# Cross network for a recommendation tower: x0 three times goes to PSUM, VectorE ends the fold, ScalarE builds the diagonals

## The chip, the cores and the metric

One core of a Trainium2 chip runs the whole kernel. The metric is the device time of one execution in microseconds (us), lower is better. The kernel before takes 761.69 us (median of three runs, 758.12 to 764.24).

## What is computed

Batch B=512, F=39 fields, D=16 embedding columns, M=128 filters per layer. Rows are gathered from 39 tables, then three cross layers multiply the input with the layer's output and contract over pairs, and a small top network follows:

```
e = stack([tbl_f[ids[:, f]] for f in range(39)], axis=1)        # 512 x 39 x 16
x0 = xk = e
for W in (f0, f1, f2):
    z = einsum('bfd,bgd->bfgd', x0, xk).reshape(b, f * g, d)
    xk = einsum('bpd,pm->bmd', z, W); outs.append(xk)
z = sum(concatenate(outs, axis=1), axis=-1)                      # 512 x 384
h = relu(concatenate([z, dense_ctx], axis=1) @ W_top1 + b_top1)
y = relu(h @ W_top2 + b_top2) @ W_top3
```

## The kernel before, in words

The 512 x 16 pairs of batch row and column d are 8192 positions, worked on in 16 **tiles** of 512 (32 batch rows each). Four tiles make a group of 128 batch rows.

**Gathers.** GpSimd gathers by indirect DMA: nine "quads" (four, three or two fields in one transfer, from a table of all small fields, `quad`, L400) per tile, and seven "singles" (`single`, L391) per group, issued in the third and fourth tile ahead of the group. SyncE stores them turned to a DRAM scratch `x0_dram` (`store_singles`, `store_quad`), then loads x0 stacked three times (`three`, `x0_three`, 117 x 512) and shifted copies of x0 into `z` (`turned_rows`), two tiles ahead.

**Layer 1** of tile t+1 is made while tile t is in layer 2, in seven chunks of three shifts each, one every fourth slot from slot 0: VectorE's `product` (L616) multiplies `z` by `x0_three`, ScalarE's `high_part` rounds the result to the matmul's type, GpSimd's `low_part` (L411) subtracts it from the product, TensorE's `contract` (L716, L717, L722) adds three matmuls per chunk into the PSUM bank `acc0`, eight slots behind the product. Then come `x1_high` and `x1_low` (L622), and the sum over d (`sum_x1`, L629).

**Layer 2** has 640 **banks**: a tile is four blocks of 128 positions, and a block ten banks (`BANKS`), one per **slot** of the code's loop. TensorE's `layer2` (L740 to L742) writes a bank of four fields x 128 filters (three in the last) to one of `RING` = 5 PSUM tensors `y2`, with three matmuls. Banks 0, 3 and 6 of each block are scaled by x0 on ScalarE (`scale_bank`, L500, four instructions), the other seven on VectorE (`add_bank`, L646, 27 instructions per block), which adds them onto one of ScalarE's three results `scaled`. TensorE may write bank n when bank n-5 has been read.

**The fold.** GpSimd adds the three parts of `scaled` (`fold_two`, L417, and the first addition of `finish_x2`, L424), halves the result twice (L426, L430) and so has `x2_sb` of the block. TensorE's `s_block` (L747) multiplies `x2_sb` by `diag`, a block-diagonal of x0 made by VectorE's `spread_rows` (L654), two instructions per tile, at slots 2 and 12. ScalarE copies the outcome to `s_sb`; `rows_of` and `rows` (L706, then L469) turn x0 to rows for it and for the scaling.

**Layer 3 and the top** of a group run on TensorE in the slots of the next group: `layer3` (L758) in slots 10 to 131 of its 160, `top1` to `top3` from slot 137 on, that is in its fourth tile. The last group's stand alone after the last bank.

Every engine's order is written out by hand in slots, and semaphores carry all dependencies. At the start `keep_warm` (L791) issues 26 matmuls that serve no result, and the two filter parts are split into high and low parts (ScalarE L469, VectorE L662, L675).

## Time and profile before

| | us |
|---|---|
| median of three runs | 761.69 |
| the profiled execution | 761.12 |
| its span, first to last instruction | 759.2 |
| around the span | 1.9 |
| first matmul of layer 2 | 49.2 |
| last bank's first matmul | 729.2 |
| mean granted TensorE clock, as a share of full speed | 0.973 |

Tile t lies between its first layer-2 matmul (L740) and the next tile's. These starts are, in us: 49.2, 97.7, 141.1, 181.4, 221.8, 267.0, 311.7, 352.4, 396.5, 441.7, 486.5, 527.2, 571.2, 612.6, 653.4, 692.3. In the profile DVE is VectorE, ACT is ScalarE, POOL is GpSimd, PE is TensorE's matmuls and PEld its weight loads. Matmuls are pipelined and each one's end is modelled, so PE's busy time overstates how little room is left.

### The profile page before, as it was taken

How to read it: one execution, taken by the hardware profiler on the slowest of the kernel's cores; microseconds unless marked ns; L12 is line 12 of the kernel's file. 1: busy time of each engine (PE TensorE's matmuls, PEld its weight loads, DVE VectorE, ACT ScalarE, POOL GpSimd, SP SyncE). 2: the span in 40 equal slices, each digit the busy share in tenths (PEclk: the TensorE clock that was granted, in tenths of full speed). 3: DMA queues.
4: the chain of work that ended last, by engine and by line, in shares of the span. 5: the costliest groups of instructions: out<-in, count | busy, mean ns of one | idle time of the engine just before them, and what ended most of it. 6: DMA issues, size and time to landing. Idle time of an engine off the chain costs nothing.

```text
span 759.2 us, 11476 instructions
## 1 busy us (share of the span) xinstructions
PE 684.3 (90%) x3058; PEld 530.7 (70%) x3058; DVE 638.4 (84%) x1981; ACT 335.4 (44%) x1019; POOL 589.1 (78%) x540
## 2 busy tenths in 40 slices
PE   0587888999999898999999898999999999999977
PEld 0365665767676676868886676877887687878856
DVE  4669798898989798998979799798969999999650
ACT  1333443544544444444544444444455454544421
POOL 6468889798989889797979979797968989574430
PEclk9979999999999999999999999999999999999989
DMA  9628220303030210303030120303031030300000
...
DMA packets 69746, 41.25 MB, mean 54 GB/s; under 512 B 46913, under 2 KB 54529, under 8 KB 69554
## 3 DMA queue, kind: packets, MB, share of 16 engines
...
q8 instruction: 24, 0.39, 0.2%
q14 instruction: 40, 0.33, 0.1%
...
## 4 chain that ended last, share of the span: by engine, by line
PE 35%; POOL 24%; DVE 24%; issue 13%; DMA 2%; SPq 1%; ACT 0%; POOLq 0%; DVEq 0%
DVE scaled L646 17%; PE y L740 7%; POOL emb_quads L400 7%; PE y L741 6%; PE y L742 6%; POOL z_parts L411 5%; POOL sum L424 4%; POOL sum L417 3%; PE late L758 3%; POOL sum L426 3%; DVE z L616 3%; PE side L747 2%; PE side L706 2%; DVE diag L654 2%; PE acc L722 2%
## 5 line engine op out<-in xcount | busy, mean ns | idle before, releaser
L646 DVE SCALAR_TENSOR_TENSOR scaled<-y,x_rows,scaled 128x128 f32<-128x128 f32 x1728 | 462.8, 338 | 72.1 <-PE y L742 49.3
L740 PE MATMUL y<-w_hi,x_parts 128*128 128x512 f32 (+1 forms) x640 | 281.9, 440 | 12.4 <-DVE scaled L646 8.6
L500 ACT ACTIVATE scaled<-y,x_rows 128x128 f32<-128x128 f32 x768 | 218.2, 367 | 149.3 <-PE y L742 148.5
L741 PE MATMUL y<-w_lo,x_parts 128*128 128x512 f32 (+1 forms) x640 | 251.4, 393 | 0.0
L742 PE MATMUL y<-w_hi,x_parts 128*128 128x512 f32 (+1 forms) x640 | 251.1, 392 | 0.0
L400 POOL DMA_INDIRECT emb_quads<-in_small_tables_dram,quad_rows x144 | 153.3, 1065 | 26.4 <-issue 18.7
L740 PEld LDWEIGHTS y<-w_hi,x_parts 128*128 128x128 f32 x640 | 122.7, 192 | 66.0 <-DVE scaled L646 42.2
L411 POOL TENSOR_TENSOR z_parts<-z,z_parts 117x512 fp32r<-117x512 f32 (+1 forms) x108 | 140.0, 1296 | 26.3 <-ACT z_parts L469 25.1
L469 ACT ACTIVATE z_parts<-z 117x512 fp32r<-117x512 f32 (+1 forms) x112 | 70.7, 632 | 162.7 <-DVE z L616 162.7
L742 PEld LDWEIGHTS y<-w_hi,x_parts 128*128 128x128 f32 x640 | 122.6, 192 | 25.2
L741 PEld LDWEIGHTS y<-w_lo,x_parts 128*128 128x128 f32 x640 | 123.4, 193 | 17.4 <-issue 0.4
L616 DVE TENSOR_TENSOR z<-z,x_three 117x512 f32<-117x512 f32 (+1 forms) x112 | 120.3, 1076 | 5.2 <-DMA z<-x_turned 5.2
L424 POOL TENSOR_TENSOR sum<-sum,scaled 128x512 f32<-128x512 f32 x64 | 88.0, 1375 | 32.8 <-DVE scaled L646 32.2
L417 POOL TENSOR_TENSOR sum<-scaled 128x512 f32<-128x512 f32 x64 | 83.0, 1297 | 36.9 <-DVE scaled L646 36.6
L722 PE MATMUL acc<-z_parts,w_hi 117*128 117x512 f32 (+1 forms) x112 | 48.8, 436 | 22.7 <-POOL z_parts L411 21.8
L758 PEld LDWEIGHTS late<-s_sb,w_sb 128*128 128x128 f32 x312 | 55.1, 200 | 11.8 <-ACT s_sb L469 1.5
L758 PE MATMUL late<-s_sb,w_sb 128*128 128x128 f32 x312 | 56.5, 285 | 0.5 <-ACT s_sb L469 0.5
L426 POOL TENSOR_TENSOR sum<-sum 128x256 f32<-128x256 f32 x64 | 52.9, 827 | 5.0
L430 POOL TENSOR_TENSOR x_sb<-sum 128x128 f32<-128x128 f32 x64 | 48.7, 761 | 9.0
L747 PE MATMUL side<-diag,x_sb 128*128 128x320 f32 x128 | 47.9, 456 | 7.8 <-issue 6.2
L469 ACT ACTIVATE s_sb<-side 128x320 f32<-128x320 f32 x64 | 27.7, 433 | 58.1 <-PE side L747 58.0
L722 PEld LDWEIGHTS acc<-z_parts,w_hi 117*128 117x128 f32 (+1 forms) x112 | 22.0, 196 | 37.6 <-POOL z_parts L411 32.1
...
## 6 DMA issues: line engine op xcount, KB each, us to landing
...
x_turned<-emb_quads SPq DMA_DIRECT2D x160, 8.0 KB
...
x_turned<-emb_singles SPq DMA_DIRECT2D x64, 2.0 KB
...
```

The lines of the kernel that those rows point to most:

```text
L400: pool.indirect_dma_start(out=emb_quads[0:SPT * n, u % 2, i, :], out_offset=None, in_=packed, in_offset=bass.IndirectOffsetOnAxis(ap=quad_ ...
L411: pool.tensor_tensor(z_lo[0:k, n % Z_RING, :], z[0:k, c, :], z_hi[0:k, n % Z_RING, :].bitcast(F32), ALU.subtract).then_inc(z_lo_in, 1)
L417: pool.tensor_tensor(sum4[:, :], scaled[:, k % 2, 0, :], scaled[:, k % 2, 1, :], ALU.add).then_inc(four_in, 1)
L424: pool.tensor_tensor(sum4[:, :], sum4[:, :], scaled[:, k % 2, 2, :], ALU.add).then_inc(four_in, 1)
L469: return act.activation(dst, src, ACT.Copy)
L500: done = act.activation(scaled[:, k % 2, BY_ACT.index(j), i * M:(i + 1) * M], y2[n % RING][:, i * M:(i + 1) * M], ACT.Copy, scale=x0_rows[ ...
L616: dve.tensor_tensor(z[0:k, c, :], z[0:k, c, :], x0_three[0:k, u % 2, :], ALU.mult).then_inc(prod, 1)
L646: dve.scalar_tensor_tensor(part, y2[n % RING][:, i * M:(i + 1) * M], x0_f, part, ALU.mult, ALU.add).then_inc(terms_in, 1)
L740: pe.matmul(dst, x1_hi[:, t % 2, cols], hi, start=True, stop=False)
L741: pe.matmul(dst, x1_hi[:, t % 2, cols], lo, start=False, stop=False)
L742: pe.matmul(dst, x1_lo[:, t % 2, cols], hi, start=False, stop=True).then_inc(y_ready, 1)
L758: mm = pe.matmul(late[:, 0:P], w2_sb[:, f, :], s_sb[:, g % 2, f, :], start=f == 0, stop=f == F - 1)
```

## The change

- **Products from PSUM.** ScalarE copies `x0_three` of a tile to a new PSUM tensor `three_ps` (`three`, at slot 38 two tiles ahead, for tile 1 at slot 2 of tile 0), and `product` multiplies `z` by it. PSUM has eight banks, so the ring `y2` has four tensors in place of five.
- **The fold.** GpSimd's two halvings go. VectorE's `x2_of` reduces `sum4` over its four parts, with one `tensor_reduce` whose inner step is 128 elements, at slot 4 of the next block.
- **Diagonals.** VectorE's `spread_rows` goes. ScalarE writes one 32-partition piece of the diagonals at each of eight slots, into one of two buffers that VectorE zeroes once.
- **Gathers.** Two singles, fields 36 and 38, become parts of quads: five singles per group. SyncE's stores per tile rise from 19 to 22.
- **The start.** `w1` is loaded ahead of `w0` (three quarters of it on ScalarE's queue), ScalarE splits `w1` first, VectorE's last two cuts of `w1_lo` come after `sum_x1(0)`, `keep_warm` issues 30, and 2 more after each of five of tile 0's contractions.

The heart of the diff:

```diff
-QUADS = ((0, 4), (5, 4), (9, 4), (13, 4), (17, 3), (21, 4), (25, 4), (29, 2), (32, 3))
-SINGLES = (4, 20, 31, 35, 36, 37, 38)
+QUADS = ((0, 1, 2, 3), (5, 6, 7, 8), (9, 10, 11, 12), (13, 14, 15, 16), (17, 18, 19, 36),
+         (21, 22, 23, 24), (25, 26, 27, 28), (29, 30, 38), (32, 33, 34))
+SINGLES = (4, 20, 31, 35, 37)
...
-RING = 5
+RING = 4
...
-FINISH_AT = 2
+THIRD_AT = 2
+X2_AT = 4
...
-DIAG_AT = (2, 12)
+THREE_AT = 38
+FIRST_THREE_AT = 2
+DIAG_AT = (1, 2, 4, 5, 7, 8, 10, 11)
...
             def fold_two(k):
                 pool.wait_ge(terms_in, dve_terms(BANKS * k + BY_ACT[2] - 1))
+                if k > 0:
+                    pool.wait_ge(x2_in, k)
                 pool.tensor_tensor(sum4[:, :], scaled[:, k % 2, 0, :], scaled[:, k % 2, 1, :],
                                    ALU.add).then_inc(four_in, 1)
...
-                pool.wait_ge(four_in, 2 * k + 2)
-                pool.tensor_tensor(sum2[:, :], sum4[:, 0:2 * M], sum4[:, 2 * M:4 * M], ALU.add).then_inc(two_in, 1)
-                if k >= 2:
-                    pool.wait_ge(s_ready, k - 1)
-                pool.wait_ge(two_in, k + 1)
-                pool.tensor_tensor(x2_sb[:, k % 2, :], sum2[:, 0:M], sum2[:, M:2 * M], ALU.add).then_inc(x2_in, 1)
...
+            def spread_rows(t, b):
+                at = slice(32 * (b // 2), 32 * (b // 2) + 32)
+                if b == 0:
+                    act.wait_ge(rows_in, t + 1)
+                    if t >= 2:
+                        act.wait_ge(s_ready, NBLK * (t - 1))
+                act.activation(diag[at, t % 2, :, b, :], x0_rows[at, t % 2, :, :], ACT.Copy,
+                               scale=mask_sb[at, b:b + 1]).then_inc(diag_in, 1)
+
+            def three(u):
+                act.wait_ge(three_in[u % 2], 48 * (u // 2 + 1))
+                if u > 0:
+                    act.wait_ge(prod, C0 * u)
+                copy(three_ps[0:3 * F, :], x0_three[0:3 * F, u % 2, :]).then_inc(three_up, 1)
...
                 if c == 0:
-                    dve.wait_ge(three_in[u % 2], 48 * (u // 2 + 1))
+                    dve.wait_ge(three_up, u + 1)
...
-                dve.tensor_tensor(z[0:k, c, :], z[0:k, c, :], x0_three[0:k, u % 2, :], ALU.mult).then_inc(prod, 1)
+                dve.tensor_tensor(z[0:k, c, :], z[0:k, c, :], three_ps[0:k, :], ALU.mult).then_inc(prod, 1)
...
+            def x2_of(k):
+                dve.wait_ge(four_in, 2 * k + 2)
+                if k >= 2:
+                    dve.wait_ge(s_ready, k - 1)
+                dve.tensor_reduce(x2_sb[:, k % 2, :], sum4[:, :].rearrange("p (f m) -> p m f", f=FPB),
+                                  AX_X, ALU.add).then_inc(x2_in, 1)
...
             pe.wait_ge(quad_in[6][0], 16)
-            keep_warm(26)
+            keep_warm(30)
             for c in range(C0):
                 contract(0, c)
-                if c == 2:
+                if c == 4:
                     rows_of(0)
+                elif c < C0 - 1:
+                    keep_warm(2)
```

GpSimd's order, in the middle of a block of layer 2, before (`z_parts` is the low part of a product, `emb_quads` a gather, `sum` and `x_sb` the fold):

```order
L411 TENSOR_TENSOR z_parts<-z,z_parts 117x512 [waits z_done,z_hi_in]
L400 DMA emb_quads<-in_small_tables_dram,quad_rows 128x16
L424 TENSOR_TENSOR sum<-sum,scaled 128x512 [waits four_in,terms_in]
L426 TENSOR_TENSOR sum<-sum 128x256 [waits four_in]
L430 TENSOR_TENSOR x_sb<-sum 128x128 [waits two_in]
```

And the same place now, with the fold of the next block's first parts after it:

```order
L426 TENSOR_TENSOR z_parts<-z,z_parts 117x512 [waits z_done,z_hi_in]
L441 TENSOR_TENSOR sum<-sum,scaled 128x512 [waits four_in,terms_in]
L415 DMA emb_quads<-in_small_tables_dram,quad_rows 128x16
L426 TENSOR_TENSOR z_parts<-z,z_parts 117x512 [waits z_done,z_hi_in]
L415 DMA emb_quads<-in_small_tables_dram,quad_rows 128x16 x2
L434 TENSOR_TENSOR sum<-scaled 128x512 [waits x2_in,terms_in]
```

The two halvings (L426, L430 before) are gone, and the next `fold_two` now also waits for VectorE's `x2_in`.

VectorE's order from the first product of a tile in steady state, before (`scaled<-y_n` is one bank, n its PSUM tensor; `z<-z` a product; `diag` the diagonals):

```order
L616 TENSOR_TENSOR z<-z,x_three 117x512
L646 SCALAR_TENSOR_TENSOR scaled<-y_1,x_rows,scaled 128x128 x4
L646 SCALAR_TENSOR_TENSOR scaled<-y_2,x_rows,scaled 128x128 x4
L654 TENSOR_TENSOR diag<-x_rows,mask_sb 128x640
L646 SCALAR_TENSOR_TENSOR scaled<-y_4,x_rows,scaled 128x128 x4
L616 TENSOR_TENSOR z<-z,x_three 117x512
L646 SCALAR_TENSOR_TENSOR scaled<-y_0,x_rows,scaled 128x128 x4
```

And now:

```order
L652 TENSOR_TENSOR z<-z,three_ps 117x512
L682 SCALAR_TENSOR_TENSOR scaled<-y_1,x_rows,scaled 128x128 x4
L682 SCALAR_TENSOR_TENSOR scaled<-y_2,x_rows,scaled 128x128 x4
L682 SCALAR_TENSOR_TENSOR scaled<-y_0,x_rows,scaled 128x128 x4
L652 TENSOR_TENSOR z<-z,three_ps 117x512
L690 TENSOR_REDUCE x_sb<-sum 128x128
L682 SCALAR_TENSOR_TENSOR scaled<-y_1,x_rows,scaled 128x128 x4
```

The diagonals are gone from VectorE, and the reduction stands behind bank 4 and its product; the PSUM tensors come round after four.

VectorE's order at the start, before (`w_lo` of 128x896 first is `w0`, the rest `w1`):

```order
L599 TENSOR_SCALAR quad_rows<-ids_four 32x15 x32
L675 TENSOR_TENSOR w_lo<-s_sb,w_hi 128x896
L662 TENSOR_TENSOR w_lo<-s_sb,w_hi 128x1024 x4
L662 TENSOR_TENSOR w_lo<-s_sb,w_hi 128x896
L616 TENSOR_TENSOR z<-z,x_three 117x512 x2
```

And now:

```order
L635 TENSOR_SCALAR quad_rows<-ids_four 32x15 x34
L706 TENSOR_REDUCE mask_sb<-ident 128x8
L708 TENSOR_TENSOR s_sb<-s_sb 128x896
L710 TENSOR_TENSOR w_lo<-s_sb,w_hi 128x896
L696 TENSOR_TENSOR w_lo<-s_sb,w_hi 128x1024 x3
L652 TENSOR_TENSOR z<-z,three_ps 117x512 x2
```

The sum of the two `w0` parts has moved behind the row numbers of the gathers, and two of the five cuts of `w1_lo` no longer stand ahead of the products.

## Rows read from the trace of the kernel before

**Rows 1.** The page's part 1: busy us, share of the span, instructions.

```profile
PE 684.3 (90%) x3058; PEld 530.7 (70%) x3058; DVE 638.4 (84%) x1981; ACT 335.4 (44%) x1019; POOL 589.1 (78%) x540
```

**Rows 2.** Windows, tiles 0, 3, 4, 5, 7, 14, 15: window, length, busy (x), clock, DMA, GB/s.

```profile
49.20:97.70 48.50, 40.21 (x155) 30.07 (x156) 40.73 (x117) 19.42 (x60) 39.09 (x38) 0.93 0.52 158
...
181.40:221.80 40.40, 38.33 (x160) 27.72 (x159) 37.99 (x121) 19.95 (x62) 36.03 (x33) 1.00 0.20 51
...
221.80:267.00 45.20, 41.63 (x176) 31.45 (x176) 39.60 (x123) 20.20 (x63) 40.18 (x38) 0.96 0.21 52
267.00:311.70 44.70, 41.48 (x184) 32.50 (x184) 39.21 (x121) 19.89 (x61) 37.62 (x35) 0.96 0.20 51
...
352.40:396.50 44.10, 44.10 (x221) 35.76 (x220) 37.90 (x119) 21.86 (x70) 35.87 (x33) 1.00 0.24 60
...
653.40:692.30 38.90, 38.66 (x185) 31.35 (x183) 37.08 (x120) 19.90 (x61) 26.26 (x23) 1.00 0.05 14
...
692.30:729.20 36.90, 36.90 (x187) 30.37 (x186) 29.57 (x109) 17.01 (x60) 14.81 (x15) 1.00 0.00 1
```

**Rows 3.** Waits within tile 5 (267.0 to 311.7 us): total us, times, longest.

```profile
PE acc L722 <- POOL z_parts L411: 2.9, 2, 2.2
...
DVE scaled L646 <- PE y L742: 3.4, 2, 1.7
```

**Rows 4.** Waits within tile 14 (653.4 to 692.3 us).

```profile
DVE scaled L646 <- PE y L742: 1.7, 1, 1.7
...
PEld y L740 <- DVE scaled L646: 0.9, 2, 0.6
```

**Rows 5.** Groups of instructions, whole span: busy us, mean ns, idle before and releaser.

```profile
L646 DVE SCALAR_TENSOR_TENSOR scaled<-y,x_rows,scaled 128x128 f32<-128x128 f32 x1728 | 462.8, 338 | 72.1 <-PE y L742 49.3 <-ACT scaled L500 22.1
...
L616 DVE TENSOR_TENSOR z<-z,x_three 117x512 f32<-117x512 f32 (+1 forms) x112 | 120.3, 1076 | 5.2 <-DMA z<-x_turned 5.2
...
L426 POOL TENSOR_TENSOR sum<-sum 128x256 f32<-128x256 f32 x64 | 52.9, 827 | 5.0
...
L430 POOL TENSOR_TENSOR x_sb<-sum 128x128 f32<-128x128 f32 x64 | 48.7, 761 | 9.0
...
L654 DVE TENSOR_TENSOR diag<-x_rows,mask_sb 128x640 f32<-128x640 f32 x32 | 35.7, 1117 | 0.0
...
L391 POOL DMA_INDIRECT emb_singles<-in_tbl_dram,ids_sb x28 | 26.9, 959 | 8.9 <-issue 5.3 <-DMA ids_sb<-in_ids_dram 2.3 <-POOL sum L417 0.8
...
L622 DVE TENSOR_TENSOR x_parts<-acc,x_parts 128x512 fp32r<-128x512 f32 x16 | 10.9, 680 | 4.0 <-ACT x_parts L469 4.0
...
L629 DVE TENSOR_REDUCE r_sb<-acc 128x32 f32<-128x512 f32 x16 | 10.9, 680 | 0.0
```

**Rows 6.** Groups of instructions, ScalarE's copy of the 156 columns of rows.

```profile
L469 ACT ACTIVATE x_rows<-side 128x156 f32<-128x156 f32 x16 | 5.2, 325 | 1.5 <-PE side L706 1.5
```

**Rows 7.** Timeline of the start: start us, length us, what, idle before.

```profile
20.90 7.22 SPq L333 DMA_DIRECT2D x_turned<-emb_quads  x14
...
25.46 8.24 PE L791 MATMUL late<-w_hi 128*128 128x512 f32 x26 [25.46 <-DMA emb_quads<-in_small_tables_dram,quad_rows]
...
34.08 0.69 DVE L616 TENSOR_TENSOR z<-z,x_three 117x512 f32<-117x512 f32 x1 [3.08 <-DMA z<-x_turned]
...
52.28 0.39 PE L741 MATMUL y<-w_lo,x_parts 128*128 128x512 f32 x1
...
55.00 0.39 PE L741 MATMUL y<-w_lo,x_parts 128*128 128x512 f32 x1
...
56.51 0.69 DVE L616 TENSOR_TENSOR z<-z,x_three 117x512 f32<-117x512 f32 x1 [1.14 <-DMA z<-x_turned]
```

**Rows 8.** Windows, 40 to 45 us, in the order of rows 2.

```profile
40.00:45.00 5.00, 4.95 (x15) 3.89 (x15) 4.18 (x5) 1.97 (x4) 4.64 (x5) 0.50 0.08 7
```

**Rows 9.** Timeline of the end.

```profile
736.77 10.45 PE L758 MATMUL late<-s_sb,w_sb 128*128 128x128 f32 x78 [0.53 <-ACT s_sb L469]
```

**Rows 10.** Waits of the whole span, ScalarE for the products.

```profile
ACT z_parts L469 <- DVE z L616: 162.7, 105, 5.8
```

More of the change, by code:

```diff
@@ L38 @@
 CHUNKS = 12500
-QUADS = ((0, 4), (5, 4), (9, 4), (13, 4), (17, 3), (21, 4), (25, 4), (29, 2), (32, 3))
-SINGLES = (4, 20, 31, 35, 36, 37, 38)
-RUNS = ((0, 1), (1, 1), (2, 1), (3, 4))
+QUADS = ((0, 1, 2, 3), (5, 6, 7, 8), (9, 10, 11, 12), (13, 14, 15, 16), (17, 18, 19, 36),
+         (21, 22, 23, 24), (25, 26, 27, 28), (29, 30, 38), (32, 33, 34))
+SINGLES = (4, 20, 31, 35, 37)
 TURNED = 20
-QUAD_STORES = tuple(i for i, (f, n) in enumerate(QUADS) for _ in range(2 if f < TURNED else 1))
-STORES = len(QUAD_STORES) + len(RUNS) + sum(1 for i, n in RUNS if SINGLES[i] < TURNED)
 GATHER_AHEAD = 14
@@ L97, with runs @@
 W1_CUTS = (0, 8, 16, 24, 32, F)
+FIRST_CUTS = 3
+def runs(fields):
+    found = []
+    for i, f in enumerate(fields):
+        if found and found[-1][1] + found[-1][2] == f:
+            found[-1][2] += 1
+        else:
+            found.append([i, f, 1])
+    return [(i, f, n, (f, F + f) if f < TURNED else (f,)) for i, f, n in found]
+STORES = sum(len(at) for q in QUADS for _, _, _, at in runs(q)) + sum(2 if f < TURNED else 1 for f in SINGLES)
 def fields_of(j):
@@ L244, in cross_network @@
         late = ps("late", [P, COLS])
+        three_ps = ps("three_ps", [P, COLS])
         ids_in = sem("ids_in")
@@ L256, in cross_network @@
         mask_in = sem("mask_in")
+        no_diag = sem("no_diag")
         w0_sum = sem("w0_sum")
@@ L456, in _ @@
                         fold_two(k)
-                    if j == FINISH_AT and k > 0:
-                        finish_x2(k - 1)
+                    if j == THIRD_AT and k > 0:
+                        fold_three(k - 1)
                     for alone, a, i in gathers_at(t, s):
@@ L463, in _ @@
                             quad(a, i)
[L464 removed]
+            fold_three(BLOCKS - 1)
         @block.scalar
@@ L539, in _ @@
             act.wait_ge(four_ids_in, 64)
-            load_filter(act, 2)
-            load_filter(act, 3)
-            act.wait_ge(w0_sum, 1)
-            copy(w0_hi[:, :, :], w0_raw).then_inc(w0_hi_in, 1)
+            for a in range(1, 4):
+                load_filter(act, a)
             act.wait_ge(w1_in, 256)
@@ L547, in _ @@
                 copy(w1_hi[:, cut, :], w1_raw[:, cut, :]).then_inc(w1_hi_in, 1)
+            act.wait_ge(w0_sum, 1)
+            copy(w0_hi[:, :, :], w0_raw).then_inc(w0_hi_in, 1)
             act.wait_ge(stored[0], 16 * STORES)
@@ L550, in _ @@
                 turned_rows(act, 0, c)
+            three(0)
             for c in range(C0):
@@ L555, in _ @@
             x1_high(0)
+            act.wait_ge(mask_in, 1)
+            act.wait_ge(blank, 1)
+            act.wait_ge(no_diag, 1)
             for t in range(TILES):
@@ L573, in _ @@
                         rows(t + 1)
+                    if s in DIAG_AT:
+                        spread_rows(t, DIAG_AT.index(s))
+                    if t == 0 and s == FIRST_THREE_AT:
+                        three(1)
+                    if t + 2 < TILES and s == THREE_AT:
+                        three(t + 2)
                     if g > 0:
@@ L594, in quad_numbers @@
             def quad_numbers(tiles):
-                for i, (f0, n) in enumerate(QUADS):
-                    for j in range(n):
+                for i, fields in enumerate(QUADS):
+                    for j, f in enumerate(fields):
                         at = slice(SPT * j, SPT * j + SPT)
-                        done = dve.tensor_scalar(quad_rows[at, tiles, i], ids_four[at, tiles, f0 + j],
-                                                 small.index(f0 + j) * CHUNKS * ROWS, None, ALU.add)
+                        done = dve.tensor_scalar(quad_rows[at, tiles, i], ids_four[at, tiles, f],
+                                                 small.index(f) * CHUNKS * ROWS, None, ALU.add)
                 return done
@@ L685, in _ @@
             sum_x1(0)
+            for i in range(FIRST_CUTS, len(W1_CUTS) - 1):
+                second_filter_low(i)
             for t in range(TILES):
@@ L697, in _ @@
                         sum_x1(t + 1)
-                    if s in DIAG_AT:
-                        spread_rows(t, DIAG_AT.index(s))
+                    if s % BANKS == X2_AT and n > BANKS:
+                        x2_of(n // BANKS - 1)
+            x2_of(BLOCKS - 1)
         @block.tensor
@@ L735, in layer2 @@
                 f = fields_of(j)
+                if n < BANKS:
+                    pe.wait_ge(w1_lo_in, sum(1 for at in W1_CUTS[:-1] if at <= f[-1]))
                 cols = slice(k % NBLK * P, k % NBLK * P + P)
```

63 lines of the change are left out of this document (24 added, 39 removed).

## The prediction, made before the changed kernel ran

> **What bounds the kernel now.** I read the page's shares first [rows 1]: TensorE is busy 90% of the span, VectorE 84%, GpSimd 78%. No engine stands out, and the share says little, since stages differ. So I cut the span into its 16 tiles [rows 2]. Tiles 3, 14 and 15 take 40.4, 38.9 and 36.9 us, tiles 4 and 5 take 45.2 and 44.7. The reader is to look at GpSimd's busy time beside the length: 36.0 of 40.4 us in tile 3, 40.2 of 45.2 in tile 4, but only 26.3 of 38.9 in tile 14, which has no gathers left to issue. Tile 14 makes a following tile and runs layer 3 like tile 5, and takes 5.8 us less. What differs is GpSimd's work: tiles 4 and 5 lie where a group's singles are gathered and quads are dense behind them. Tile 7 is another case: TensorE is busy for all of it (44.1 of 44.1), because the top network is added there.
>
> How GpSimd's lateness reaches the others is seen in the waits of tile 5 [rows 3]: TensorE waits 2.9 us for a low part of a product, and VectorE then waits 3.4 us for TensorE. After such a gap TensorE's granted clock is 0.96 as the mean of tiles 4 and 5, that is, a piece of them runs at 1.2 GHz and not 2.4 GHz; in tiles 3 and 14 it is 1.00 [rows 2]. In tile 14 VectorE waits 1.7 us only [rows 4]. So tiles 1 to 6, 8 to 10, 12 and 13 are bound by GpSimd together with VectorE, tiles 7 and 11 by TensorE, tile 14 by VectorE (37.1 busy of 38.9) with TensorE close behind, tile 15 by TensorE.
>
> **GpSimd's part of the change.** The two halvings go: 0.83 + 0.76 us per block [rows 5], 6.4 us per tile for four blocks; about 101.6 us in all. Two singles in seven go too: 0.96 us each [rows 5], 8 in all. Tile 3's 36.0 us fall to 29.6, tile 4's 40.2 to some 33. Both are then far under the tile's length, so GpSimd's low parts come in time, as in tile 14. Its new wait, `fold_two` for the reduction of the block before, is free if that reduction at slot 4 comes ahead of slot 8; behind it in GpSimd's queue stand low parts and gathers.
>
> **VectorE's part.** Per tile it loses its two diagonals: 2 x 1.12 = 2.2 us [rows 5]. Its products take 1.08 us in the mean, though the subtraction L622, with one of its two inputs in PSUM and the same 512 columns, takes 0.68 [rows 5]; the first product of tile 0, before GpSimd's first low part, takes 0.69 too [rows 7]. I take the rest for a wait for GpSimd on the way to SBUF, and since the new product has one input in PSUM, 0.68: 7 x 0.40 = 2.8 us less (bounds: 0 if that reading is wrong, 2.8). It gains four reductions. The trace has no reduction with an inner step of 128 elements; L629, the same 512 elements in order from PSUM, takes 0.68 us [rows 5]. Lower bound 0.6 (the row less its overlap with the instruction before), upper bound twice the row, 1.36; I take the row's 0.68: 2.7 us more. Sum: 2.2 + 2.8 - 2.7 = 2.3 us less per tile. Tile 14 has no gathers to be in its products' way, so I take half the saving, 1.4, there: 37.1 - 2.2 - 1.4 + 2.7 leaves 36.2 us.
>
> The Trainium skill's page "Vector Engine (DVE) Microarchitecture Reference", section "Measured stream behaviour on trn2" with its paragraph "The SBUF access granule: adjacent pairs", speaks against this reduction: a port keeps its full rate only where consecutive elements come as adjacent pairs, and a stream that hops at every element costs 1.73 to 2.5 ns per column. An estimate from that page is 0.96 to 1.36 us for the 512 columns here, and by it the sum would be 4 x 0.28 = 1.1 to 4 x 0.68 = 2.7 us worse per tile. No row here shows it; it is the first rival's mechanism.
>
> **ScalarE's part.** It gains eight diagonal pieces of 160 columns, each at most the 0.33 us of its copy of 156 columns [rows 6], 2.6 us, and one copy of 512 columns, about 0.63 us. Its busy time goes from 19.9 to 23.1 us of a tile of about 39: hidden, because it mostly waits. Cost taken 0; up to 0.3 us for each piece that stands ahead of a scaled bank VectorE needs, 1 us per tile, at the upper end.
>
> **TensorE and the ring.** TensorE's own need: from one L741 at 52.28 to the one four banks on at 55.00 us lie 12 matmuls, 0.23 us each at full clock [rows 7]. Of the 120 layer-2 matmuls of a tile 12 have only 384 columns: 108 x 0.23 + 12 x 0.17 = 26.9 us; 21 for the contraction 4.8; transposes and diagonals about 3; layer 3 26 x 0.13 = 3.5 at most (78 take 10.5 in the tail [rows 9]). That is 34.7 without layer 3 and 37 to 38 with it. A ring of four leaves TensorE one bank less of lead. Not shown before; bounded by 0 and one bank of 0.7 us for each of a tile's seven products, 4.9 us; I take 0.2, near the lower end, since four banks are still 3.0 us of VectorE's work (a bank is 4 instructions of 462.8 / 1728 = 0.27 us [rows 5], and seven banks in ten are its own) and the disturbances (one product, one reduction, one contraction) are 0.7 us each.
>
> **The start.** Layer 2 begins at 49.2 us. TensorE contracts tile 0 at half clock (0.50 from 40 to 45 us [rows 8]), and the products begin at 34.08 [rows 7]. The new order saves GpSimd two gathers ahead of the quads, but splits `w0` last, so `keep_warm` can only begin at about 27 (an estimate: the quads are in at 25.46 [rows 7] and the loads with them, and two splits of some 1 us follow) and, with 30 matmuls after the 26 that took 8.24 us [rows 7], end near 36. Seven contractions of 0.7 us and the extra matmuls of 0.46 give 44, then 1.3 us for the x1 parts: layer 2 begins near 45.5. Much of that is lost again, since tile 1's data set the pace: the first product of tile 1, at 56.5 and waiting for its DMA [rows 7], cannot come much sooner than two or three microseconds less, and now ScalarE stands at slot 2 for the stacked x0 and does bank 3 behind it. I take 54.8. SyncE's three more stores cost 0 to 1.5 us here (7.22 us for 14 [rows 7]) and are in it. The rest of tile 0 took 97.7 - 56.5 = 41.2 and falls like a loaded tile, to 36.5: tile 1 begins at 91.3 instead of 97.7.
>
> **The sum.** Tiles 1 to 3 (no layer 3): 38.1 each, VectorE's 36 us and the 2 us by which tile 14 exceeds its bound; 114.3. The nine tiles 4 to 6, 8 to 10 and 12 to 14: tile 14's 38.9 as it stands, with all of VectorE's saving there given to TensorE's need, plus 0.2 for the ring, 39.1 each; 351.9. Tiles 7 and 11: 43.5 each, as TensorE bounds them; 87.0. Tile 15: 36.8. Together 590.0, against 631.5 before. The tail from the last bank, 30.0 us, has one reduction of 0.68 in place of two halvings, whose means together are 1.59 but which nothing disturbs there: 29.8. So 91.3 + 590.0 + 29.8 = 711.1 us of span, and with 1.9 around it 713.0, against 761.12 of the profiled execution. That execution stands 0.6 us under the median of 761.69, which is nothing: 713.
>
> **Rivals.** *The reduction on VectorE takes the place of GpSimd's work* (0.17). Either it is slow by its stride, or VectorE stands at slot 4 until GpSimd's second addition is done. For it: both engines are full in the first 26 slots of a tile. Against it: from a block's last term to the reduction VectorE has three banks, over 3 us, and GpSimd needs 1.3 for its addition. What stands behind the waiting reduction are banks 5 to 9 of the next block, for whose release TensorE's ring waits, and the next product, for which ScalarE waits. 
>
> *GpSimd was not the bound* (0.10): its waits are symptoms and only VectorE's 2.3 us and the start count: 761 - 16 x 1.5 = 737 with TensorE taking part of it.
>
> *The ring of four decides, and it gets slower* (0.05). ScalarE waits 105 times for a product [rows 10], 1.55 us each, and a bank of its own is stuck behind each wait. If, with one PSUM tensor fewer, TensorE stood one bank, 0.7 us, at each, that is 74 us: 713 + 74 = 787. It decides from 48 / 105 = 0.46 us per wait on. Against it: in tile 14, where VectorE is nearly full, TensorE's loads wait 0.9 us in all for its releases [rows 4]. The Trainium skill's "TensorE: Matmul & The Clock Gate", in "A second HAM failure mode: psum-queue depth-cycling", reports that small stalls from cycling PSUM banks let the clock swing between its levels; of the tiles 3, 4, 5, 7 and 14, with the same ring, it was lower only in 4 and 5 [rows 2].
>
> *The loads come late* (0.06): the copy to `three_ps` waits at slot 38 for its DMA in each tile. SyncE's chain is 3 stores longer, but GpSimd's gathers come sooner. Behind the copy stands bank 0 of the next tile, which VectorE's bank 1 needs. 1 us for each of 14 tiles: 727.
>
> **How the numbers follow.** The forecast has 0.62. The lower end is TensorE's need alone in the nine tiles (38 instead of 39.1, 10 us) and 0.6 us less in the others (4 us), a start 2 us better: 713 - 10 - 4 - 2 = 697. The upper end takes in the first, second and fourth rivals with some of the ring: 741. A difference under 1% is about what a measurement of this kernel cannot tell from none: faster by more 0.92 (the forecast and all rivals but that of the ring, less 0.03 of their tails), within 0.05 and slower 0.03 (the ring's case, half of it milder than its price, and those tails).
>
> **What would show it.** Right: GpSimd busy about 30 us per tile; products at 0.68 us; tiles 4 and 5 as long as tile 12; clock 1.00 in them; no wait of TensorE for L411's successor. Wrong: a reduction over 0.9 us or a VectorE wait on GpSimd's sum in front of it (first rival); TensorE waiting for VectorE's or ScalarE's releases several us per tile instead of tile 14's 0.9 (third); tiles 4 and 5 still longer than 12 (second); ScalarE waiting for `x_three` (fourth).

## The result and the profile after

The changed kernel takes 734.37 us (median of four runs, 733.42 to 735.52), the kernel before beside it 760.22. The ratio is 0.9654, with a 95% interval of 0.9623 to 0.9686: 3.5% faster. Forecast were 713.0 us within 697 to 741.

The page's part 1 of the changed kernel, against [rows 1]:

```profile
PE 671.3 (91%) x3072; PEld 523.1 (71%) x3072; DVE 626.0 (85%) x2018; ACT 390.5 (53%) x1163; POOL 459.2 (63%) x404
```

GpSimd's share fell from 78% to 63%, ScalarE's rose from 44% to 53%, and TensorE and VectorE are each a point fuller. By tile, the windows of the changed kernel (tiles 0, 3, 4, 5, 7, 14 and 15, columns as in [rows 2]):

```profile
54.10:99.90 45.80, 38.87 (x156) 29.05 (x156) 38.03 (x121) 23.44 (x70) 34.93 (x32) 0.93 0.55 162
...
176.20:215.20 39.00, 37.91 (x159) 27.51 (x158) 37.55 (x122) 23.14 (x70) 28.64 (x26) 1.00 0.22 51
215.20:255.10 39.90, 38.96 (x176) 30.15 (x176) 37.79 (x122) 23.69 (x71) 30.83 (x28) 1.00 0.21 48
255.10:294.90 39.80, 39.23 (x184) 31.43 (x184) 37.61 (x122) 23.37 (x70) 28.79 (x26) 1.00 0.25 58
...
334.60:380.30 45.70, 45.13 (x220) 35.51 (x219) 37.76 (x122) 25.43 (x78) 28.51 (x26) 1.00 0.21 51
...
625.10:664.80 39.70, 39.22 (x185) 31.48 (x183) 37.45 (x122) 22.89 (x69) 19.03 (x16) 1.00 0.01 2
664.80:704.20 39.40, 38.59 (x188) 29.84 (x187) 32.99 (x114) 20.17 (x68) 9.54 (x9) 1.00 0.00 1
```

Tiles 4 and 5 took 45.2 and 44.7 us and now take 39.9 and 39.8, as long as tile 14, and the clock in them is 1.00, not 0.96. GpSimd is busy for 31 and 29 of these 40 us. So far that is the forecast, but for 0.6 to 0.8 us per tile (39.1 was forecast). And tile 14 got longer (38.9 to 39.7), tile 7 from 44.1 to 45.7 and tile 15 from 36.9 to 39.4, and tile 0 begins at 54.1 us, not 49.2. The groups of instructions, against [rows 5] and [rows 6]:

```profile
L682 DVE SCALAR_TENSOR_TENSOR scaled<-y,x_rows,scaled 128x128 f32<-128x128 f32 x1728 | 465.4, 342 | 53.5 <-PE y L781 35.6 <-ACT scaled L526 17.2
...
L441 POOL TENSOR_TENSOR sum<-sum,scaled 128x512 f32<-128x512 f32 x64 | 83.1, 1299 | 36.8 <-DVE scaled L682 36.3
...
L652 DVE TENSOR_TENSOR z<-z,three_ps 117x512 f32<-117x512 f32 (+1 forms) x112 | 75.6, 677 | 0.0
...
L690 DVE TENSOR_REDUCE x_sb<-sum 128x128 f32<-128x512 f32 x64 | 68.7, 1073 | 2.3 <-POOL sum L441 2.1
...
L496 ACT ACTIVATE diag<-x_rows,mask_sb 32x160 f32<-32x160 f32 x128 | 48.6, 416 | 1.2
...
L480 ACT ACTIVATE three_ps<-x_three 117x512 f32<-117x512 f32 x16 | 9.9, 617 | 7.8 <-DMA x_three<-x_turned 7.8
```

The product fell from 1.08 to 0.68 us, as forecast. The reduction L690 takes 1.07 us, not 0.68, and a diagonal piece L496 0.42, not 0.33. From the waits of tile 15 of the changed kernel (TensorE's weight loads waiting for VectorE: us in all, times, the longest):

```profile
PEld y L779 <- DVE scaled L682: 3.4, 8, 0.9
```

The same wait in tile 15 of the kernel before:

```profile
PEld y L740 <- DVE scaled L646: 0.2, 1, 0.2
```

TensorE's weight loads, which hardly waited for VectorE there (0.2 us), now wait 3.4 us. And the start of the changed kernel, from the timeline, against [rows 7]:

```profile
20.65 6.26 DVE L635 TENSOR_SCALAR quad_rows<-ids_four 32x15 int32<-32x15 int32 x34 [10.98 <-DMA ids_four<-in_ids_dram]
...
26.94 0.29 DVE L706 TENSOR_REDUCE mask_sb<-ident 128x8 f32<-128x128 f32 x1
...
33.42 9.39 PE L830 MATMUL late<-w_hi 128*128 128x512 f32 x30 [33.42 <-DVE w_lo L710]
...
49.17 0.30 ACT L480 ACTIVATE x_rows<-side 128x156 f32<-128x156 f32 x1 [4.93 <-PE side L743]
...
54.31 2.21 DVE L696 TENSOR_TENSOR w_lo<-s_sb,w_hi 128x1024 fp32r<-128x1024 f32 x2
```

VectorE stands until 20.65 us for the ids of the other tiles, whose load now lies behind a quarter of `w1`; the first sum and splits of `w0` are behind its 34 small additions, so the 30 matmuls begin at 33.42 (25.46 before). At 49.17 ScalarE has waited 4.9 us for the transposes, with the last two chunks of tile 0 queued behind them. Then, in tile 0 (ScalarE, then VectorE):

```profile
62.38 0.60 ACT L480 ACTIVATE three_ps<-x_three 117x512 f32<-117x512 f32 x1 [5.52 <-DMA x_three<-x_turned]
```

```profile
64.15 1.13 DVE L682 SCALAR_TENSOR_TENSOR scaled<-y,x_rows,scaled 128x128 f32<-128x128 f32 x4 [5.55 <-ACT scaled L526]
65.19 0.68 DVE L652 TENSOR_TENSOR z<-z,three_ps 117x512 f32<-117x512 f32 x1
```

ScalarE waits 5.5 us at slot 2 for tile 1's stacked x0, bank 3 comes after it, and VectorE waits 5.6 us for bank 3: the first product of tile 1 starts at 65.2 us, against 56.5 before.

The span is 733.7 us where 711.1 was forecast, 22.6 us more. Tile 1 begins at 99.9 instead of 91.3 (8.6 us more); tiles 1 to 3 take 115.3 instead of 114.3 (1.0); the nine tiles with layer 3, 39.66 to 39.92 each, 358.2 instead of 351.9 (6.3); tiles 7 and 11 together 91.4 instead of 87.0 (4.4); tile 15 39.4 instead of 36.8 (2.6); the tail 29.5 instead of 29.8.

### The profile page after: what moved, and what is told of

Its sections match the earlier page's. It is cut to its first block, busy times and chain, and to the rows that moved or that the text cites. A ratio compares the mean times of both kernels' runs of the same rounds, so it can differ in the third digit from the quotient of the medians.

```text
span 733.7 us, 11667 instructions
## 1 busy us (share of the span) xinstructions
PE 671.3 (91%) x3072; PEld 523.1 (71%) x3072; DVE 626.0 (85%) x2018; ACT 390.5 (53%) x1163; POOL 459.2 (63%) x404
## 4 chain that ended last, share of the span: by engine, by line
PE 67%; DVE 19%; issue 5%; DMA 3%; POOL 2%; ACT 2%; ACTq 1%; SPq 0%; DVEq 0%; POOLq 0%
PE y L779 17%; PE y L781 14%; PE y L780 14%; DVE scaled L682 14%; PE late L797 4%; PE side L786 3%; PE acc L754 3%; PE acc L753 3%; PE acc L759 3%; PE side L743 2%; DMA s_sb<-in_w_dram 2%; PE late L808 2%; DVE z L652 1%; PE late L830 1%; DVE x_parts L658 1%
## 5 line engine op out<-in xcount | busy, mean ns | idle before, releaser
L779 PE MATMUL y<-w_hi,x_parts 128*128 128x512 f32 (+1 forms) x640 | 277.7, 434 | 18.2 <-DVE scaled L682 8.8
L781 PE MATMUL y<-w_hi,x_parts 128*128 128x512 f32 (+1 forms) x640 | 249.0, 389 | 0.0
L780 PE MATMUL y<-w_lo,x_parts 128*128 128x512 f32 (+1 forms) x640 | 248.6, 389 | 0.0
L426 POOL TENSOR_TENSOR z_parts<-z,z_parts 117x512 fp32r<-117x512 f32 (+1 forms) x108 | 139.5, 1291 | 88.8 <-ACT z_parts L480 67.1
L779 PEld LDWEIGHTS y<-w_hi,x_parts 128*128 128x128 f32 x640 | 120.8, 189 | 80.8 <-DVE scaled L682 50.6
L415 POOL DMA_INDIRECT emb_quads<-in_small_tables_dram,quad_rows x144 | 138.0, 959 | 32.7 <-issue 15.5
L781 PEld LDWEIGHTS y<-w_hi,x_parts 128*128 128x128 f32 x640 | 120.7, 189 | 24.9
L441 POOL TENSOR_TENSOR sum<-sum,scaled 128x512 f32<-128x512 f32 x64 | 83.1, 1299 | 36.8 <-DVE scaled L682 36.3
L652 DVE TENSOR_TENSOR z<-z,three_ps 117x512 f32<-117x512 f32 (+1 forms) x112 | 75.6, 677 | 0.0
L690 DVE TENSOR_REDUCE x_sb<-sum 128x128 f32<-128x512 f32 x64 | 68.7, 1073 | 2.3 <-POOL sum L441 2.1
L496 ACT ACTIVATE diag<-x_rows,mask_sb 32x160 f32<-32x160 f32 x128 | 48.6, 416 | 1.2
L753 PE MATMUL acc<-z_parts,w_hi 117*128 117x512 f32 (+1 forms) x112 | 44.4, 396 | 0.9 <-ACT z_parts L480 0.9
L759 PE MATMUL acc<-z_parts,w_hi 117*128 117x512 f32 (+1 forms) x112 | 44.2, 395 | 0.7 <-POOL z_parts L426 0.7
```

Of the source, the lines that this page charges most:

```text
L415: pool.indirect_dma_start(out=emb_quads[0:SPT * n, u % 2, i, :], out_offset=None, in_=packed, in_offset=bass.IndirectOffsetOnAxis(ap=quad_ ...
L426: pool.tensor_tensor(z_lo[0:k, n % Z_RING, :], z[0:k, c, :], z_hi[0:k, n % Z_RING, :].bitcast(F32), ALU.subtract).then_inc(z_lo_in, 1)
L441: pool.tensor_tensor(sum4[:, :], sum4[:, :], scaled[:, k % 2, 2, :], ALU.add).then_inc(four_in, 1)
L652: dve.tensor_tensor(z[0:k, c, :], z[0:k, c, :], three_ps[0:k, :], ALU.mult).then_inc(prod, 1)
L779: pe.matmul(dst, x1_hi[:, t % 2, cols], hi, start=True, stop=False)
L780: pe.matmul(dst, x1_hi[:, t % 2, cols], lo, start=False, stop=False)
```

## The experiments

Theory A is the forecast's with its sizes mended: GpSimd's work bound the kernel, its removal is what pays, and the slow reduction, the ring of four and the new start give part of it back. The rivals are named in the expectations. The twelve kernels ran in three groups of four (1 to 4, 5 to 8, 9 to 12), each group beside the kernel before, whose medians were 757.87, 758.38 and 760.57 us. A ratio is to that median.

### 1. The ring alone, on the kernel before

```diff
-RING = 5
+RING = 4
```

> The kernel before with a ring of four PSUM tensors in place of five, nothing else. Theory A (the ring costs little, TensorE's lead of four banks is enough): 761 to 766 us. Theory B (the ring of four is what keeps the changed kernel above the forecast, since tiles 7 and 15 became 1.7 and 2.5 us longer there): 15 to 35 us more than before, about 775 to 795.

Measured: 755.62 us, ratio 0.9962 (0.9937 to 0.9987): 0.4% less, outside both expectations. The windows of its tiles 4, 14 and 15, and a wait within tile 15, show two effects of opposite sign:

```profile
219.70:263.30 43.60, 40.07 (x176) 29.78 (x175) 39.58 (x122) 20.23 (x63) 39.97 (x38) 1.00 0.20 46
646.50:686.10 39.60, 39.00 (x185) 31.47 (x183) 37.05 (x120) 20.09 (x61) 26.23 (x23) 1.00 0.05 14
686.10:723.70 37.60, 37.53 (x189) 29.93 (x187) 29.87 (x109) 17.00 (x59) 14.55 (x16) 1.00 0.00 1
```

```profile
PEld y L740 <- DVE scaled L646: 1.4, 5, 0.5
```

Tile 14 takes 39.6 (38.9 before) and tile 15 37.6 (36.9), and tiles 7 and 11 take 44.7 (44.0): 0.7 us more in each of the four tiles in which TensorE or VectorE and not GpSimd is the bound; in tile 15 TensorE's loads wait 1.4 us for VectorE, against 0.2. But tile 4 takes 43.6 in place of 45.2, at a clock of 1.00 and not 0.96 [rows 2]. That gain goes with the clock: in executions with the same mean clock both kernels take about the same time (spans of 753.1 to 754.9 us with four tensors and 753.7 with five at 0.984; 756.4 and 754.1 to 756.6 at 0.980), as far as these few executions tell; but with four tensors the mean clock was 0.980 to 0.989, and 0.966 to 0.982 with five beside it. How the ring acts on the clock was not tried. So theory B falls as the explanation of the 20 us. The 0.7 us per tile are real, and the changed kernel, whose clock is 1.00 from tile 1 to tile 15, has no such gain to set against them.

### 2. GpSimd's halvings alone

The fold's last addition of 512 columns goes straight to a buffer, and the diagonals multiply its first 128 columns; three quarters of x2 are left out.

```diff
-                pool.tensor_tensor(sum4[:, :], sum4[:, :], scaled[:, k % 2, 2, :], ALU.add).then_inc(four_in, 1)
-                pool.wait_ge(four_in, 2 * k + 2)
-                pool.tensor_tensor(sum2[:, :], sum4[:, 0:2 * M], sum4[:, 2 * M:4 * M], ALU.add).then_inc(two_in, 1)
+                pool.tensor_tensor(x2_sb[:, k % 2, :], sum4[:, :], scaled[:, k % 2, 2, :], ALU.add).then_inc(four_in, 1)
...
-                pool.tensor_tensor(x2_sb[:, k % 2, :], sum2[:, 0:M], sum2[:, M:2 * M], ALU.add).then_inc(x2_in, 1)
```

> The kernel before without GpSimd's two halvings, the diagonals multiply the first quarter of the sum (this leaves out three quarters of the block's x2). Theory A (GpSimd bound tiles 1 to 6, 8 to 10, 12 and 13): tiles 4 and 5 fall from 45 to about 41 us, the time falls by 20 to 30 us to about 735. Theory C (GpSimd's waits were only symptoms): within 5 us of before.

Measured: 712.83 us, ratio 0.9382 (0.9345 to 0.9419). That is 45 us, one and a half times the upper end of what I expected and more than the whole change brought. Its tiles 4 and 5, and its products:

```profile
206.60:246.50 39.90, 38.73 (x177) 30.60 (x177) 38.28 (x123) 20.23 (x63) 33.70 (x29) 1.00 0.20 48
246.50:286.00 39.50, 38.66 (x184) 31.43 (x183) 37.79 (x121) 19.91 (x61) 31.34 (x27) 1.00 0.23 58
```

```profile
L614 DVE TENSOR_TENSOR z<-z,x_three 117x512 f32<-117x512 f32 (+1 forms) x112 | 100.1, 895 | 4.0 <-DMA z<-x_turned 3.9
```

Tiles 4 and 5 are 5.3 and 5.2 us shorter than [rows 2], with VectorE's diagonals still there, the ring still five and the products still from SBUF. Of tile 4's 5.3 us, 1.6 are what it lost in experiment 1 too, where its clock rose to 1.00, and VectorE is busy for 1.3 us less (39.6 to 38.3), since its products fell to 0.90 us in the mean by themselves; the trace behind experiment 6 shows why. TensorE's wait for a low part in tile 5, 2.9 us in [rows 3], is gone. So GpSimd's halvings held the kernel up in two ways, by coming ahead of its low parts and by lengthening VectorE's products. Theory C falls; the two ways were not taken apart.

### 3. The reduction with neighbouring elements

Wrong elements are added; their number, the output and the waits stay.

```diff
-                dve.tensor_reduce(x2_sb[:, k % 2, :], sum4[:, :].rearrange("p (f m) -> p m f", f=FPB),
+                dve.tensor_reduce(x2_sb[:, k % 2, :], sum4[:, :].rearrange("p (m f) -> p m f", f=FPB),
```

> The changed kernel, with VectorE's reduction reading four neighbouring elements for each result in place of four that lie 128 apart (so the wrong elements are added). Theory A (the inner step makes the reduction 1.07 us and not 0.68): the reduction takes 0.6 to 0.7 us, and the time falls by 5 to 20 us. Theory D (the reduction is slow because its input is in SBUF or for its 128 results): it stays at 1.07 us and the time at 734.

Measured: 721.21 us, ratio 0.9512 (0.9479 to 0.9546), 13.2 us under the changed kernel by the medians.

```profile
L690 DVE TENSOR_REDUCE x_sb<-sum 128x128 f32<-128x512 f32 x64 | 43.3, 677 | 2.1 <-POOL sum L441 1.8
```

```profile
PEld y L779 <- DVE scaled L682: 2.0, 5, 0.6
```

The first line is the reduction: 0.68 us, as the row of L629 in [rows 5]. The inner step alone made the difference, theory D falls. The second is the wait of TensorE's loads within tile 15, 2.0 us and not 3.4. VectorE had 64 x 0.40 = 25 us less to do, half of which reached the time: tiles 2 and 3 lost 1.6 us each, the nine with layer 3, where TensorE is nearly full, 0.5 to 0.6.

### 4. The loads and splits of before

The order of SyncE's and ScalarE's loads, of the sums and splits is that of the kernel before; `keep_warm` stays as changed.

```diff
-            load_filter(sp, 0)
...
+            load_filter(sp, 0)
+            load_filter(sp, 1)
...
-            for a in range(1, 4):
-                load_filter(act, a)
+            load_filter(act, 2)
+            load_filter(act, 3)
+            act.wait_ge(w0_sum, 1)
+            copy(w0_hi[:, :, :], w0_raw).then_inc(w0_hi_in, 1)
```

> The changed kernel with the loads and splits of the filters in the order of before (w0 first, all five cuts of w1_lo ahead of the products); keep_warm stays at 30 and 2. Theory A (the new order makes the start late, through the row numbers and the last split of w0): layer 2 begins at 45 to 49 us in place of 54.1 and the time falls by 3 to 8 us. Theory E (the start is bound by the gathers and stores): layer 2 begins at 52 to 54 and the time stays.

Measured: 735.24 us, ratio 0.9685 (0.9651 to 0.9719), the same as the changed kernel, as theory E had it. The start in its profile, then the window from 40 to 44 us:

```profile
25.99 9.15 PE L828 MATMUL late<-w_hi 128*128 128x512 f32 x30 [25.99 <-DVE w_lo L711]
36.40 0.60 ACT L481 ACTIVATE three_ps<-x_three 117x512 f32<-117x512 f32 x1 [7.19 <-DMA x_three<-x_turned]
38.44 0.80 PE L751 MATMUL acc<-z_parts,w_hi 117*128 117x512 f32 x1 [3.30 <-ACT z_parts L481]
```

```profile
40.00:44.00 4.00, 4.00 (x10) 3.13 (x10) 3.89 (x7) 1.86 (x3) 2.86 (x3) 0.50 0.33 56
```

The 30 matmuls begin 7.4 us sooner, but the stacked x0 of tile 0 lands only at 36.4, so the contractions begin at 38.4 (42.65 in the changed kernel). TensorE has stood for 3.3 us before them, and its granted clock from 40 to 44 us is 0.50, where the changed kernel has 1.00. With the wait for the transposes behind it, layer 2 begins at 52.7 us and tile 1 at 97.3, 1.4 and 2.6 us sooner; the tail gives 2.0 back (31.6 us against 29.6). The order of the loads alone is not the cause.

### 5. and 6. Products from SBUF, with a ring of four and of five

```diff
-                dve.tensor_tensor(z[0:k, c, :], z[0:k, c, :], three_ps[0:k, :], ALU.mult).then_inc(prod, 1)
+                dve.tensor_tensor(z[0:k, c, :], z[0:k, c, :], x0_three[0:k, u % 2, :], ALU.mult).then_inc(prod, 1)
```

and ScalarE's `three` with its waits gone (SyncE's load of `x0_three` waits for the products again, as in the kernel before); in the second also `RING = 5`.

> The changed kernel with the products reading x0 from SBUF as before (no copy to PSUM), ring of four kept. Theory A (with two inputs in SBUF a product waits for GpSimd, the less the emptier GpSimd is): products 0.85 to 0.95 us as in the run without the halvings (0.90), VectorE 1.5 us per tile busier, 738 to 750 us. Theory F (the copy to PSUM brings nothing once GpSimd has room): 734 or less.

> The same with a ring of five, the PSUM tensor freed by the missing copy. Theory A (the ring of four costs 0.7 us in each tile that TensorE bounds, as tiles 7, 14 and 15 of the kernel before with a ring of four show): 5 to 11 us under the run with four. Theory F, the copy is a bad trade for the fifth tensor: below 734 us. Theory A says the two nearly cancel: 730 to 742.

Measured: 752.59 us with four (0.9918, 0.9883 to 0.9953) and 744.66 with five (0.9798, 0.9754 to 0.9842). Both are slower than I expected at most (750 and 742) and worse than the changed kernel. The copy to PSUM is worth 18 us at equal ring, and the fifth tensor takes 8 of them back. In the groups of the run with four, the product and GpSimd's second addition:

```profile
L641 DVE TENSOR_TENSOR z<-z,x_three 117x512 f32<-117x512 f32 (+1 forms) x112 | 100.3, 897 | 1.7 <-DMA z<-x_turned 1.7
L440 POOL TENSOR_TENSOR sum<-sum,scaled 128x512 f32<-128x512 f32 x64 | 88.3, 1380 | 37.3 <-DVE scaled L671 36.7
```

With two SBUF inputs the product takes 0.90 us in the mean in place of 0.68, and GpSimd's additions suffer as well: 1.38 in place of 1.30. The mean hides two kinds of product. One of each from tile 5 of that run, with what GpSimd does at the time:

```profile
267.99 0.68 DVE L641 TENSOR_TENSOR z<-z,x_three 117x512 f32<-117x512 f32 x1
285.41 2.62 DVE L641 TENSOR_TENSOR z<-z,x_three 117x512 f32<-117x512 f32 x1
```

```profile
284.92 1.31 POOL L425 TENSOR_TENSOR z_parts<-z,z_parts 117x512 fp32r<-117x512 f32 x1
286.17 1.30 POOL L440 TENSOR_TENSOR sum<-sum,scaled 128x512 f32<-128x512 f32 x1
```

Of the run's 112 products, the 49 that overlap no addition or subtraction of GpSimd take 0.67 to 0.69 us. The 30 that take over 0.8 us overlap one, all of them. In the kernel before 76 of 112 take over 0.8, in the run without the halvings 40, and again all of these overlap one. In the changed kernel, whose products have one input in PSUM, 72 overlap such an instruction, and none takes more than 0.70. The Trainium skill's "SBUF — State Buffer", in "Who interferes with whom", says that a VectorE instruction with two SBUF inputs contends with a GpSimd instruction that reads SBUF. By that rule, the trace agrees.

The loss is not even. The profiled span is 15.2 us longer than that of the changed kernel, and tiles 1, 5 and 9 (41.8, 43.4 and 43.4 us, against 37.4, 39.8 and 39.8) have 11.6 of it: there some products meet two of GpSimd's instructions in a row, as above. The other tiles are at most 0.8 us longer.

### 7. The sum written transposed

```diff
-                pool.tensor_tensor(sum4[:, :], sum4[:, :], scaled[:, k % 2, 2, :], ALU.add).then_inc(four_in, 1)
+                pool.tensor_tensor(sum4_m[:, :].rearrange("p (m f) -> p f m", f=FPB),
+                                   sum4[:, :].rearrange("p (f m) -> p f m", f=FPB),
+                                   scaled[:, k % 2, 2, :].rearrange("p (f m) -> p f m", f=FPB),
+                                   ALU.add).then_inc(four_in, 1)
```

VectorE reduces `sum4_m` with neighbouring elements.

> The changed kernel, but GpSimd's second addition writes its sum with the four parts of a result side by side, so that VectorE's reduction reads neighbouring elements and the right ones are added. Theory A (only the inner step made the reduction slow; GpSimd has room for a slower write): reduction 0.68 us, time 719 to 724 us. Theory G (GpSimd's writes with a step of four elements take twice as long and VectorE waits for them): above 726.

Measured: 722.23 us, ratio 0.9518 (0.9482 to 0.9555).

```profile
L442 POOL TENSOR_TENSOR sum_m<-sum,scaled 128x512 f32<-128x512 f32 x64 | 83.9, 1311 | 36.4 <-DVE scaled L686 36.0
...
L694 DVE TENSOR_REDUCE x_sb<-sum_m 128x128 f32<-128x512 f32 x64 | 43.4, 678 | 2.1 <-POOL sum_m L442 1.8
```

The write with a step of four elements costs GpSimd nothing to speak of (1.31 us, 1.30 in the changed kernel), and the reduction takes 0.68. Theory G falls.

### 8. Two additions in place of the reduction

```diff
-                dve.tensor_reduce(x2_sb[:, k % 2, :], sum4[:, :].rearrange("p (f m) -> p m f", f=FPB),
-                                  AX_X, ALU.add).then_inc(x2_in, 1)
+                dve.tensor_tensor(sum2[:, :], sum4[:, 0:2 * M], sum4[:, 2 * M:4 * M], ALU.add).then_inc(two_in, 1)
+                dve.wait_ge(two_in, k + 1)
+                dve.tensor_tensor(x2_sb[:, k % 2, :], sum2[:, 0:M], sum2[:, M:2 * M], ALU.add).then_inc(x2_in, 1)
```

> The changed kernel with VectorE's reduction replaced by two additions, 256 and 128 columns. Theory A: 0.40 and 0.27 us with some waits for GpSimd since both inputs are in SBUF, together 0.7 to 1.0 us against 1.07, time 722 to 732. Theory G (waits for GpSimd eat it): 734 or more.

Measured: 734.68 us, ratio 0.967 (0.9632 to 0.9708), no gain. The two additions:

```profile
L692 DVE TENSOR_TENSOR sum<-sum 128x256 f32<-128x256 f32 x64 | 43.9, 686 | 1.5 <-POOL sum L443 1.4
...
L694 DVE TENSOR_TENSOR x_sb<-sum 128x128 f32<-128x128 f32 x64 | 20.1, 314 | 2.2
```

Together 1.00 us, against 1.07. Two of the first additions, and GpSimd's instruction beside the second:

```profile
301.76 0.42 DVE L692 TENSOR_TENSOR sum<-sum 128x256 f32<-128x256 f32 x1
310.59 1.63 DVE L692 TENSOR_TENSOR sum<-sum 128x256 f32<-128x256 f32 x1
```

```profile
310.63 1.30 POOL L428 TENSOR_TENSOR z_parts<-z,z_parts 117x512 fp32r<-117x512 f32 x1
```

49 of the 64 take 0.41 to 0.42 us and overlap no addition or subtraction of GpSimd; the other 15 take 1.33 to 1.66, and each overlaps one. So theory G is right: an addition with two inputs in SBUF costs little by itself, and meeting GpSimd eats the gain.

### 9. and 10. The transposes sooner, and the whole start of before

```diff
-                if c == 4:
+                if c == 2:
                     rows_of(0)
                 elif c < C0 - 1:
                     keep_warm(2)
```

and, in the second, the order of experiment 4 with `keep_warm(26)` and no matmuls between the contractions.

> The changed kernel with TensorE's transposes of tile 0 after the third contraction instead of the fifth, and so with no extra matmuls behind the third but two behind the fifth. Theory A (ScalarE stands 4.9 us for these transposes, and the last two chunks are queued behind them): layer 2 begins 1 to 3 us sooner than 54.1, the time falls by as much at most. Theory H (the start is bound by the late row numbers and the 30 matmuls of keep_warm that begin at 33.4): no change.

> The changed kernel with the whole start of before: loads, splits, 26 matmuls of keep_warm, none between the contractions, transposes after the third. Theory A (the new start costs, by its order, its 14 extra matmuls and the later transposes): layer 2 begins at 47 to 50 us, tile 1 at 93 to 96, and the time is 727 to 731. Theory E (tile 1's data set the pace, whatever tile 0 does): tile 1 begins at 97 or later and the time is 732 to 735.

Measured: 733.72 us (0.9656, 0.9604 to 0.9708) and 731.25 (0.962, 0.9567 to 0.9674). In their profiles layer 2 begins at 50.8 and 49.7 us and tile 1 at 95.1 and 92.8, where the changed kernel has 54.1 and 99.9. The start of the second:

```profile
24.84 8.56 PE L828 MATMUL late<-w_hi 128*128 128x512 f32 x26 [24.84 <-DMA emb_quads<-in_small_tables_dram,quad_rows]
...
43.36 0.30 ACT L481 ACTIVATE x_rows<-side 128x156 f32<-128x156 f32 x1 [2.31 <-PE side L741]
...
49.66 0.47 PE L777 MATMUL y<-w_hi,x_parts 128*128 128x512 f32 x1 [1.62 <-DVE x_parts L659]
```

So moving one call (and with it one pair of the extra matmuls) gains 3.3 us at layer 2's start and 4.8 at tile 1's, and the whole start of before 4.4 and 7.1. Not all of the 3.3 is the call's, though: in that one profile the 30 matmuls begin at 31.8 us, against 33.4, since the ids of the other tiles landed 1.7 us sooner (18.9 us; 20.3 to 20.9 in four other profiles with the same order of loads). That leaves some 1.7 us for the call. The medians fell by 0.7 and 3.1 us only. Part of the rest is in the tail, where the second's profile gives 2.3 us back: first the changed kernel's tail, then this one's.

```profile
704.20:733.70 29.50, 20.32 (x135) 17.33 (x135) 3.76 (x12) 3.31 (x11) 2.52 (x2) 0.88 0.00 1
```

```profile
697.60:729.40 31.80, 22.62 (x135) 19.53 (x135) 3.78 (x12) 3.33 (x11) 2.54 (x2) 0.84 0.00 1
```

The same 135 matmuls, but at a mean clock of 0.84 in place of 0.88. Over the fourteen profiles the tail takes 28.7 to 30.0 us in the six whose clock there is 0.88 to 0.94, and 30.8 to 31.8 in the eight at 0.83 or 0.84; the tails of experiments 4, 8 and 9 are among these, 31.5 to 31.7. What decides between them was not tried, so a gain of 2 us ahead of the tail may or may not reach the time.

### 11. and 12. Together

> Transposed write of GpSimd's sum and the whole start of before together. If the two act apart (theory A): 722 less what the start alone gives, 715 to 719 us. Theory E: 720 to 723.

> The same without the copy to PSUM and with a ring of five. The copy is worth 18 us and the ring takes 8 of it back in the kernel with the slow reduction. Theory A (both are the same with the short reduction, since VectorE is less full, the copy is worth less): 718 to 728, no better than with the copy. Theory I (VectorE has now enough room that the fifth tensor outweighs the copy): below 715.

Measured: the transposed sum with the start of before, 718.30 us, ratio 0.9441 (0.9388 to 0.9494); without the copy to PSUM and with a ring of five, 723.05, ratio 0.9516 (0.9462 to 0.9569). The first computes all of the network and is the fastest version that does, 16 us under the changed kernel. The copy is worth 4.8 us against the fifth tensor even with the short reduction; theory I falls.

## Why the prediction was right, and where its sizes were off

The time, 734 us, lies in the range, and the way and the main cause were forecast. But the range of 44 us took in three of the rivals, and the fall was 26 us where 48 was forecast. 734 is the price of the first rival, 735, and its sign, a reduction over 0.9 us, did appear. That the two numbers agree is luck in part: the rival put all 22 us on the reduction, which cost 13, and the rest came from the start and from the tiles that TensorE bounds.

*GpSimd bound most tiles*: right, and shown by experiment 2, where its halvings alone were worth 45 us. The rival "GpSimd was not the bound" is out. GpSimd acted in two ways, by its late low parts and by lengthening VectorE's products, and the prediction had both, the second as a term of its own. That tiles 4 and 5 would become what tile 14 is held to 0.2 us (39.9 and 39.8 beside 39.7).

*VectorE's products, 0.68 us from PSUM*: right (0.677). Of the fall from 1.08, nearly half (to 0.90) comes with GpSimd's emptier queue alone, experiments 2 and 5. At equal ring the copy is worth 18 us. The reading behind the term, a wait for GpSimd, is shown by the single products in experiment 6.

*"Lower bound 0.6, upper bound twice the row, 1.36; I take the row's 0.68"*: this is the first term that was mis-sized. It measured 1.07 us, so VectorE's saving was 2.3 - 1.6 = 0.7 us per tile, and by experiment 3 the term is worth 13 us of the 21 by which 713 was short. The first rival's mechanism was at work, by its stride and not by its wait: VectorE waited for GpSimd's sum 2.1 us in the whole span. The Trainium skill's "Vector Engine (DVE) Microarchitecture Reference", in "Measured stream behaviour on trn2", had given 1.73 to 2.5 ns per column for a stream that hops at every element, an estimate of 0.96 to 1.36 us here. The trace agrees with 1.07 us, and without the hops, in experiment 3, it is 0.68. I had cited it and gone by the row that was near in shape but not in stride.

*"I take 0.2, near the lower end", for the ring*: 0.7 us in each tile that TensorE bounds, experiment 1. My argument, four banks of VectorE's work against disturbances of one, looked at whether VectorE runs dry; what the rows of tile 15 show is the other side, TensorE waiting for releases: 0.2 us before, 1.4 with the ring of four alone, 3.4 in the changed kernel and 2.0 in it with the short reduction. Tiles 7, 14 and 15 of the changed kernel are thus longer than before: of tile 15's 2.5 us, 0.7 come with the ring, 1.0 with the reduction (38.35 in experiment 3), and 0.8 are not assigned.

*"Layer 2 begins near 45.5", "tile 1 begins at 91.3"*: wrong by 8.6 us both (54.1 and 99.9). I had `keep_warm` at 27 us; it began at 33.4, since I didn't follow the ids of the other tiles, moved behind a quarter of `w1`, into VectorE's queue ahead of the `w0` sum. Experiment 4 shows that this step cost only 1.4 us at layer 2 and 2.6 at tile 1, for in its profile the contractions wait for the stacked x0 and then run at half clock. About as much came from the later transposes, which stand in ScalarE's queue ahead of the last two chunks and which I overlooked: experiment 9 gives back 3.3 and 4.8 us, some 1.6 of each by ids that landed sooner in that profile. ScalarE's stop at slot 2 for tile 1's x0 took 5.5 us, and the first product of tile 1 began at 65.2, not at the 54.8 that I had. Experiment 10 gives back 7.1 us at tile 1 and 3.1 in the median. What each piece is worth in the time was not taken apart.

The last two terms overlap with the first and with each other, so they don't add up to the 21 us exactly.

Of the other rivals, "the ring of four decides" is out: alone it made the kernel before no slower. "The loads come late" happened once: of the 7.8 us that ScalarE waited for the stacked x0 in the whole span, 5.5 are the stop in tile 0.

*ScalarE's work is hidden*: it is busy 23 of 40 us, though a piece took 0.42 us where at most 0.33 was forecast. No run takes its pieces away, so that they cost nothing is argued and not shown.
